# A decoder layer on one core: the mixer's steps regrouped, its last two steps written out with early output products

## The chip, the cores and the metric

The kernel runs on one core of a Trainium2 chip. The metric is the device time of one execution in microseconds. Every time below comes from the time measurements or from one profiled execution.

## The reference, cut to what matters

One decoder layer on x of 4 sequences of 256 tokens with 256 channels: a state-space mixer, an expert layer chosen by token id (weights from ctx), a mixture of 16 experts with two picks a token, each followed by a residual and a layer norm. The change lies in the mixer and its output projection:

```
proj = x @ Win.T                      # per head: x 64, z 64, B 128, C 128 columns, and dt
xc, Bc, Cc = silu(causal_conv(...))   # 4 taps
dt = softplus(dt_raw + dt_bias); decay = exp(-dt * exp(A_log))
h_t = decay_t * h_(t-1) + dt_t * xc_t (x) Bc_t ;  y_t = h_t . Cc_t     # 32 heads
y = y * rsqrt(mean(y * y) + 1e-6) * silu(z)
x = layernorm(x + y.reshape(B, T, 2048) @ Wout.T)
```

## The kernel before, in words

**Work and tiles.** The 32 heads are taken in 16 pairs. A pair n has six tiles of 128 projection channels: tile 0 is x of both heads, tiles 1 to 4 are B and C of the first and of the second head, tile 5 is z. All 1024 tokens run through a tile in two halves of 512. So PE has twelve tiles-and-halves per pair, numbered j = 0 to 11 (in the text: a tile of six matmuls each, since an fp32 product is made of three fp32r products for two slices of 128 channels; `project`, L689). They rotate over four PSUM banks (j % 4).

**Stages.** ACT copies each half out of PSUM times the last tap (`copy`, L1101); DVE adds the other taps from PSUM (`tap`, L1401; three small ones per half in tile 0, two large and two small ones in tiles 1 to 4); a bank is free for tile j + 4 after the tap with shift 3 of that half, which is what `project` waits for (`half_read`). ACT applies silu (L1086), and to the z tile directly from PSUM (L1092). The recurrence is done as products inside chunks: PE turns x to tokens (`x_to_tokens`, L674, four transposes a clump), DVE scales it by dt (`x_scaled`, L1376), PE makes eight scores B C per pair (`score`, L703 and L704), POOL builds the logarithms of the decay (`log_decay`, L421 and L427), ACT exponentiates them (`exp_decay`, L1107), DVE multiplies score and decay (`weigh`, k = 0 to 7, L1385), and PE multiplies that by x (`mix`, L717, four per pair). A score k waits for weigh k - 2, whose bank it uses. The mean of squares: ACT squares (L1112, L1113), POOL makes the low part (`low_part`, L441), PE averages (`mean_square`, L726 and L727, per half g), ACT takes the root (`rsqrt`, L1118 and L1120), DVE applies the gate (`gate`, L1409), POOL normalises into y_all (`norm`, L436).

**Pipeline of steps.** Step n projects pair n (`front`), does x, scores and the mix of the first half for pair q = n - 1 (`mid`), and the second half's mix and both norms for pair r = n - 2 (`tail`). Steps 0 and 1 fill it, steps 2 to 15 have all three (a loop of seven rounds of two), step 16 has mid and tail, step 17 tail alone. Each engine runs its own list in order, and the lists are written out by hand: on PE a dictionary says which other work stands behind which j (L734 to L756), on ACT `work[j]`, on DVE `between[(tile, tap)]`, on POOL the body of `step` (L443). The work between two tiles on PE is a clump below.

**Behind the steps.** SP loads woutT into wo_sb when the last projection is done (L320), the ids and x later (L328, L333). ACT splits the weight into wo_hi (L1176) and makes y_high of pairs 0 to 3 (L1171), DVE finds the owners by id and makes wo_lo (L1557) and y_low of those four (L1562). PE multiplies output blocks 0 and 1 in fp32 (`out_project`, L634), 16 products each, of which the last needs pair 15; then `project_half` makes the blocks 4 to 7 at once from high and low parts (L652, 96 matmuls), six matmuls for each pair i in order. For pairs from 4 on ACT makes y_high and POOL y_low (L506) as it goes. `normed` layer norms, the expert layers and the router follow; they are not touched.

## Time and profile before

| what | us |
|---|---|
| runs shown: median (lowest to highest) of 3 | 718.29 (716.29 to 718.94) |
| the profiled execution: time | 716.46 |
| the profiled execution: span | 714.70 |
| ACT: copy, silu, exponential, one square, Ln and Exp of a root, table load | 0.69, 1.06, 0.84, 0.60, 0.68 and 0.63, 1.28 |
| POOL: log decay of one sequence (two of 0.83, one of 1.29), low part, norm | 2.9, 1.29, 1.29 |
| POOL: split of the next pair's weights | 2.75 and 3.53 |
| POOL: constants, first to last | 4.6 |
| DVE: four y_low (L1562) | 2.5 |

The durations are means of one instruction. A row of the timeline gives the start and the duration in us; a start-to-start distance is the time that an instruction really takes from its engine, since matmuls, and to a small extent the operations of ACT, DVE and POOL, lie over their successors. An fp32 product stands as two records.

### The profile page before, as it was taken

How to read it: one execution, taken by the hardware profiler on the slowest of the kernel's cores; microseconds unless marked ns; L12 is line 12 of the kernel's file. 1: busy time of each engine (PE TensorE's matmuls, PEld its weight loads, DVE VectorE, ACT ScalarE, POOL GpSimd, SP SyncE). 2: the span in 40 equal slices, each digit the busy share in tenths (PEclk: the TensorE clock that was granted, in tenths of full speed). 3: DMA queues.
4: the chain of work that ended last, by engine and by line, in shares of the span. 5: the costliest groups of instructions: out<-in, count | busy, mean ns of one | idle time of the engine just before them, and what ended most of it. 6: DMA issues, size and time to landing. Idle time of an engine off the chain costs nothing.

```text
span 714.7 us, 11631 instructions
## 1 busy us (share of the span) xinstructions
PE 652.1 (91%) x3364; PEld 503.0 (70%) x3364; DVE 539.9 (76%) x856; ACT 451.9 (63%) x744; POOL 478.2 (67%) x452
## 2 busy tenths in 40 slices
PE   6689999999999999999999999899989998999920
PEld 3467777777777777877877777687867775777710
DVE  4879999999999999999999999739525484222236
ACT  3366797797797887877877877865224554333321
POOL 4065887887987888889779876656425758762034
PEclk9899999999999999999999999999999999999975
DMA  4311311311311211112122110320345924543124
GB/s 150 125 46 60 104 46 60 103 45 59 103 45 59 94 54 59 56 66 84 45 63 99 45 59 0 118 95 16 95 118 138 356 73 103 161 136 95 53 74 132
DMA packets 25474, 62.32 MB, mean 87 GB/s; under 512 B 5206, under 2 KB 18134, under 8 KB 22710
## 3 DMA queue, kind: packets, MB, share of 16 engines
q1 hardware_dynamic: 22278, 53.31, 22.1%
q0 software_dynamic: 3168, 8.67, 4.9%
q8 instruction: 14, 0.23, 0.1%
q14 instruction: 14, 0.11, 0.1%
HBM read 52.77 MB, written 9.20 MB: 87 GB/s over the span
## 4 chain that ended last, share of the span: by engine, by line
PE 80%; DVE 7%; POOL 6%; issue 3%; ACT 2%; DMA 2%; POOLq 0%; SPq 0%; DVEq 0%; ACTq 0%
PE ps L689 35%; PE ps L703 8%; PE ps L717 6%; PE ps L934 5%; PE ps L974 4%; PE ps L704 4%; PE ps L634 3%; DVE conv L1401 3%; PE ps L652 2%; POOL conv L599 2%; PE ps L674 2%; PE ps L726 1%; PE ps L952 1%; PE ps L822 1%; PE ps L727 1%
## 5 line engine op out<-in xcount | busy, mean ns | idle before, releaser
L1401 DVE SCALAR_TENSOR_TENSOR conv<-ps,w_raw,conv 128x506 f32<-128x506 f32 (+3 forms) x352 | 324.7, 935 | 19.6 <-ACT conv L1101 13.4
L689 PE MATMUL ps<-x_hi,w_hi 128*128 128x512 f32 x384 | 166.2, 433 | 9.9 <-DVE conv L1401 8.3
L1101 ACT ACTIVATE conv<-ps,w_raw 128x512 f32<-128x512 f32 x160 | 109.8, 687 | 100.2 <-PE ps L689 98.5
L689 PE MATMUL ps<-x_hi,w_lo 128*128 128x512 f32 x384 | 152.1, 396 | 0.0
L689 PE MATMUL ps<-x_lo,w_hi 128*128 128x512 f32 x384 | 151.6, 395 | 0.0
L421 POOL TENSOR_TENSOR decay<-cum_b,cum_tok 128x512 f32<-128x512 f32 (+1 forms) x128 | 103.6, 833 | 24.2 <-DVE cum_tok L1365 24.2
L689 PEld LDWEIGHTS ps<-x_hi,w_hi 128*128 128x128 f32 x384 | 73.3, 191 | 35.1 <-DVE conv L1401 20.5
L427 POOL TENSOR_TENSOR decay<-decay,mask 128x512 f32<-128x512 f32 x64 | 82.8, 1294 | 5.0
L689 PEld LDWEIGHTS ps<-x_hi,w_lo 128*128 128x128 f32 x384 | 72.9, 190 | 16.7
L689 PEld LDWEIGHTS ps<-x_lo,w_hi 128*128 128x128 f32 x384 | 73.5, 191 | 10.3
L703 PE MATMUL ps<-conv 128*128 128x256 f32 x256 | 78.0, 386 | 2.7 <-DVE xs L1376 2.1
L1385 DVE TENSOR_TENSOR decay<-ps,decay 128x384 f32<-128x384 f32 x128 | 69.2, 550 | 14.2 <-PE ps L704 12.4
L1086 ACT ACTIVATE conv<-conv 128x1024 f32<-128x1024 f32 x80 | 79.5, 1064 | 0.0
L441 POOL TENSOR_TENSOR y_lo<-y_sq,y_hi 128x512 fp32r<-128x512 f32 x32 | 41.4, 1292 | 52.6 <-ACT y_sq L1113 52.6
L436 POOL TENSOR_TENSOR y_all<-z_gate,y_all 128x512 f32 (+1 forms) x32 | 41.1, 1285 | 28.6 <-ACT y_all L1120 28.6
L703 PEld LDWEIGHTS ps<-conv 128*128 128x128 f32 x256 | 44.2, 189 | 14.5 <-DVE decay L1385 4.2
L1107 ACT ACTIVATE decay<-decay 128x768 f32<-128x768 f32 x64 | 53.9, 843 | 0.1
L411 POOL TENSOR_TENSOR w_lo<-w_raw,w_hi 128x1536 fp32r<-128x1536 f32 x15 | 52.9, 3529 | 1.2
L704 PEld LDWEIGHTS ps<-conv 128*128 128x128 f32 x256 | 48.6, 190 | 6.7
L717 PE MATMUL ps<-decay,xs 128*64 128x256 f32 (+1 forms) x512 | 49.0, 333 | 1.2 <-DVE decay L1385 1.2
L704 PE MATMUL ps<-conv 128*128 128x128 f32 x256 | 49.2, 274 | 0.0
L717 PEld LDWEIGHTS ps<-decay,xs 128*64 128x64 f32 x512 | 31.7, 136 | 21.7 <-issue 10.6
(233 smaller groups left out, 1065.1 us busy)
## 6 DMA issues: line engine op xcount, KB each, us to landing
cum_b<-cum_scratch SPq DMA_DIRECT2D x16, 1024.0 KB, 4.7
w_raw<-in_winT SPq DMA_DIRECT2D x16, 778.0 KB, 4.3
y_all<-in_wgu SPq DMA_DIRECT2D x4, 1408.0 KB, 19.3
ys_scratch<-y_blk SPq DMA_DIRECT2D x31, 128.0 KB, 1.8
late<-in_wdn SPq DMA_DIRECT2D x2, 1408.0 KB
x_scratch<-conv SPq DMA_DIRECT2D x19, 128.0 KB, 6.6
late<-in_woutT SPq DMA_DIRECT2D x1, 2048.0 KB, 8.3
res_scratch<-conv SPq DMA_DIRECT2D x11, 128.0 KB, 1.9
```

Of the source, the lines that this page charges most:

```text
L411: pool.tensor_tensor(w_lo[:, par, :], raw, w_hi[:, par, :].bitcast(F32), ALU.subtract).then_inc(S["w_split"], 1)
L421: pool.tensor_tensor(decay[:, 2 * b:2 * b + 2, c:t], cum_b[:, qp, :, b * T + j * P:(b + 1) * T], cum_tok[:, 2 * b + j, bass.ds(q * 2, 2)]. ...
L427: pool.tensor_tensor(diag, diag, mask[:, :].unsqueeze(1).unsqueeze(1).broadcast_to([P, 2, 2, P]), ALU.add).then_inc(S["p_arg"], 1)
L689: mm = pe.matmul(ps[:, j % 4, :], wp[:, par, w], xp[:, kk, t], start=(i == 0), stop=(i == 5))
L703: pe.matmul(ps[:, 4 + k % 2, 0:T], Bm[:, c0:c0 + P], Cm[:, c0:c0 + T], start=True, stop=True)
L704: pe.matmul(ps[:, 4 + k % 2, T:SC], Bm[:, c1:c1 + P], Cm[:, c1:c1 + P], start=True, stop=True).then_inc(S["s_done"], 1)
L717: mm = pe.matmul(ps[ch, 6 + g, (b % 2) * T + j * P:(b % 2) * T + T], xs[:, 2 * b + j, ch], decay[:, 2 * b + h, c:t], start=(j == 0), stop= ...
L1086: act.activation(conv[:, pp, tile, :], conv[:, pp, tile, :], ACT.Silu).then_inc(S["a_silu"], 1)
L1101: act.activation(conv[:, par, tile, hf * 512:(hf + 1) * 512], ps[:, j % 4, :], ACT.Copy, scale=w_raw[:, par, tap:tap + 1]).then_inc(S["a_c ...
L1107: act.activation(d, d, ACT.Exp).then_inc(S["a_decay"], 1)
L1385: dve.tensor_tensor(decay[:, k, :], ps[:, 4 + k % 2, 0:SC], decay[:, k, :], ALU.mult).then_inc(S["v_m"], 1)
L1401: dve.scalar_tensor_tensor(out=o[:, :, s:], in0=u[:, :, 0:T - s], scalar=w_raw[:, par, c:c + 1], in1=o[:, :, s:], op0=ALU.mult, op1=ALU.ad ...
```

## The change

- PE's clumps in steps with front: behind j = 0 mean square 0; 1 transposes 0, both mixes of r; 3 transposes 1, mean square 1; 4 scores 0 and 1; 6 score 2; 7 scores 3 and 4; 9 scores 5 and 6, both mixes of q, score 7.
- ACT, DVE and POOL lists of these steps are put in another order to match.
- Steps 16 and 17 get lists of their own. Six of the sixteen products of output blocks 0 and 1 (`project_early`) go between the scores of step 16, with their weights in `wo_early`, a second copy of the first six row blocks of woutT in w_raw's first half, loaded once pair 14 has left it. w_sh's load waits for these products. The other products up to pair 14 stand at the start and in the middle of step 17.
- wo_hi and y_high of pairs 0 to 3 move on ACT into step 16, owners by id and wo_lo on DVE too, and POOL's constants ahead of its step 17. ACT's second of two loads of the logarithm's table there goes.

```diff
+            sp.wait_ge(S["v_tap"], (NPAIR - 1) * TAP_N)
+            sp.wait_ge(S["w_split"], 2 * (NPAIR - 1))
+            sp.dma_start(wo_early, woutT[0:EARLY_WO * P, :].rearrange("(i p) d -> p i d", p=P)).then_inc(S["ld_early"], 16)
...
+            sp.wait_ge(S["eo_done"], 2)
...
+                if isinstance(n, int) and n >= NPAIR:
+                    if mid:
+                        log_decay(n - 1, 1 - par, 2)
+                    low_part(n - 2, 1)
+                    if mid:
+                        log_decay(n - 1, 1 - par, 3)
+                    norm(n - 2, par, 0)
+                    norm(n - 2, par, 1)
+                    if mid:
+                        low_part(n - 1, 0)
+                    return
+                if tail:
+                    low_part(n - 2, 1)
+                    norm(n - 2, par, 0)
                 if mid:
                     log_decay(n - 1, 1 - par, 2)
-                if tail:
-                    low_part(n - 2, 1)
-                if mid:
                     log_decay(n - 1, 1 - par, 3)
-                if tail:
-                    norm(n - 2, par, 0)
                 if split_next:
                     split(n + 1, 1 - par)
+                if mid:
+                    low_part(n - 1, 0)
                 if tail:
                     norm(n - 2, par, 1)
...
+            def project_early(b, first, end):
+                if b == 0 and first == 0:
+                    pe.wait_ge(S["ld_early"], 16)
+                    pe.wait_ge(S["v_tap"], NPAIR * TAP_N)
+                for i in range(first, end):
+                    mm = pe.matmul(ps[:, b, 0:D], y_all[:, i, b * P:(b + 1) * P], wo_early[:, i, :],
+                                   start=(i == 0), stop=False)
+                if end == EARLY_WO:
+                    mm.then_inc(S["eo_done"], 1)
...
-                for j in range(2 * NTILE):
-                    if front:
-                        project(j)
+                def between_tiles(j):
+                    if tail and j == 0:
+                        mean_square(r, 0)
+                    if mid and j in (1, 3):
+                        x_to_tokens(j // 2)
                     if tail and j == 1:
                         mix(r, 2)
                         mix(r, 3)
-                        mean_square(r, 0)
-                        if isinstance(n, int) and n == NPAIR + 1:
-                            pe.wait_ge(S["a_z"], 2 * NPAIR)
-                            out_project(0, 0, NPAIR - 1)
-                    if mid and j in (1, 2):
-                        x_to_tokens(j - 1)
+                    if tail and j == 3:
+                        mean_square(r, 1)
                     if mid:
-                        for k in {3: (0,), 5: (1, 2)}.get(j, ()):
+                        for k in {4: (0, 1), 6: (2,), 7: (3, 4), 9: (5, 6)}.get(j, ()):
                             score(k)
-                    if tail and j == 5:
-                        mean_square(r, 1)
-                    if mid and j == 8:
+                    if mid and j == 9:
                         mix(q, 0)
                         mix(q, 1)
-                    if mid:
-                        for k in {5: (3,), 6: (4,), 9: (5,), 10: (6, 7)}.get(j, ()):
-                            score(k)
+                        score(7)
+                if front:
+                    for j in range(2 * NTILE):
+                        project(j)
+                        between_tiles(j)
+                    return
+                if mid:
+                    x_to_tokens(0)
+                    mix(r, 2)
+                    mix(r, 3)
+                    mean_square(r, 0)
+                    x_to_tokens(1)
+                    project_early(0, 0, EARLY_WO // 2)
+                    score(0)
+                    score(1)
+                    project_early(0, EARLY_WO // 2, EARLY_WO)
+                    score(2)
+                    score(3)
+                    project_early(1, 0, EARLY_WO // 2)
+                    mean_square(r, 1)
+                    mix(q, 0)
+                    score(4)
+                    mix(q, 1)
+                    score(5)
+                    project_early(1, EARLY_WO // 2, EARLY_WO)
+                    score(6)
+                    score(7)
+                    return
+                pe.wait_ge(S["a_z"], 2 * NPAIR)
+                out_project(0, EARLY_WO, NPAIR - 1)
+                mean_square(r, 0)
+                mix(r, 2)
+                mix(r, 3)
+                out_project(1, EARLY_WO, NPAIR - 1)
+                mean_square(r, 1)
...
+                if not front:
+                    if mid:
+                        silu(q, qp, 4)
+                        z(0)
+                        z(1)
+                        act.preload_act_table_set("natural_log_exp_and_others")
+                        exp_decay(0)
+                    square(r, 1)
+                    if mid:
+                        exp_decay(1)
+                    rsqrt(r, 0)
+                    if mid:
+                        exp_decay(2)
+                        exp_decay(3)
+                    rsqrt(r, 1)
+                    if mid:
+                        square(q, 0)
+                        act.wait_ge(S["ld_wo"], 16)
+                        for c in range(4):
+                            part = slice(4 * c, 4 * c + 4)
+                            act.activation(wo_hi[:, part, :], wo_sb[:, part, :], ACT.Copy).then_inc(S["a_wo"], 1)
+                        for i in range(YRING):
+                            high_y(i)
+                    return
                 if mid:
-                    z(0)
-                    work[0] += [lambda: z(1), lambda: silu(q, qp, 4)]
+                    work[0] += [lambda: z(0), lambda: silu(q, qp, 4)]
+                    work[1] += [lambda: z(1)]
                 if isinstance(n, int) and n == 0:
                     work[0] += [lambda: softplus(0)]
                     work[1] += [lambda: softplus(1), lambda: softplus(2)]
                     work[2] += [lambda: softplus(3)]
-                if mid or tail:
-                    work[1] += [lambda: act.preload_act_table_set("natural_log_exp_and_others")]
                 if tail:
                     work[1] += [lambda: square(r, 1)]
-                    work[4] += [lambda: rsqrt(r, 0)]
+                    work[3] += [lambda: rsqrt(r, 0)]
+                if mid:
+                    work[1] += [lambda: act.preload_act_table_set("natural_log_exp_and_others")]
+                    for b, j in enumerate((4, 4, 6, 7)):
+                        work[j] += [lambda b=b: exp_decay(b)]
+                if tail:
                     work[6] += [lambda: rsqrt(r, 1)]
-                if mid:
-                    for b, j in enumerate((1, 2, 7, 8)):
-                        work[j] += [lambda b=b: exp_decay(b)]
-                if front:
-                    work[8] += [lambda: act.preload_act_table_set("silu_and_others")]
+                work[9] += [lambda: act.preload_act_table_set("silu_and_others")]
                 if mid:
                     work[9] += [lambda: square(q, 0)]
...
+                if not front:
+                    if mid:
+                        x_scaled(0)
+                        x_scaled(1)
+                        weigh(0)
+                    gate(r, rp, 1)
+                    if mid:
+                        for k in range(1, 7):
+                            weigh(k)
+                        gate(q, qp, 0)
+                        weigh(7)
+                        owners_by_id()
+                        for c in range(4):
+                            dve.wait_ge(S["a_wo"], c + 1)
+                            part = slice(4 * c, 4 * c + 4)
+                            dve.tensor_tensor(wo_lo[:, part, :], wo_sb[:, part, :], wo_hi[:, part, :].bitcast(F32), ALU.subtract
+                                              ).then_inc(S["v_wo"], 1)
+                    return
                 between = {}
+                if mid:
+                    between[0, 5] = [lambda: x_scaled(0)]
                 if isinstance(n, int) and n == 0:
                     between[1, 0] = [sum_dt]
-                if mid:
-                    between[1, 0] = [lambda: x_scaled(0)]
                 if tail:
                     between.setdefault((1, 0), []).append(lambda: gate(r, rp, 1))
                 if mid:
-                    between[1, 0] += [lambda: x_scaled(1), lambda: weigh(0)]
-                    for k, at_ in ((1, (1, 3)), (2, (2, 0)), (3, (3, 0)), (4, (3, 2)), (5, (4, 0))):
-                        between[at_] = [lambda k=k: weigh(k)]
-                    between[4, 3] = [lambda: gate(q, qp, 0)]
+                    between.setdefault((1, 0), []).append(lambda: x_scaled(1))
+                    for k, at_ in enumerate(((2, 0), (2, 0), (2, 2), (2, 3), (3, 1), (3, 2))):
+                        between.setdefault(at_, []).append(lambda k=k: weigh(k))
                 for m in range(NCONV):
                     for i in range(len(TAPS_OF[m])):
                         for f in between.get((m, i), []):
                             f()
-                        if front:
-                            tap(m, i)
+                        tap(m, i)
                 if mid:
+                    gate(q, qp, 0)
                     weigh(6)
                     weigh(7)
```

## Rows read from the trace of the kernel before

**Rows 1.** The page's totals: busy us, share of the span, instructions.
```profile
PE 652.1 (91%) x3364; PEld 503.0 (70%) x3364; DVE 539.9 (76%) x856; ACT 451.9 (63%) x744; POOL 478.2 (67%) x452
```
**Rows 2.** Stretches: busy us by engine, PEclk, DMA share, GB/s.
```profile
311.40:338.88 27.48, 27.45 (x150) 21.47 (x148) 26.03 (x35) 22.15 (x32) 22.77 (x19) 1.00 0.20 67
455.05:486.92 31.87, 28.62 (x165) 23.19 (x165) 16.07 (x29) 22.53 (x32) 22.49 (x29) 1.00 0.37 119
486.92:510.06 23.14, 22.61 (x96) 18.03 (x97) 17.61 (x29) 8.26 (x16) 16.87 (x15) 1.00 0.03 12
```
**Rows 3.** Waits within one loop step, 311.4 to 338.88: total, times, longest.
```profile
PEld ps L689 <- DVE conv L1401: 0.8, 2, 0.5
```
**Rows 4.** Timeline of PE in a loop step: start, us, operation.
```profile
326.26 0.59 PE L703 MATMUL ps<-conv 128*128 128x256 f32 x2
...
326.83 0.47 PE L689 MATMUL ps<-x_hi,w_hi 128*128 128x512 f32 x1
...
329.67 0.59 PE L703 MATMUL ps<-conv 128*128 128x256 f32 x2
...
330.32 0.60 PE L703 MATMUL ps<-conv 128*128 128x256 f32 x2
...
331.47 0.70 PE L703 MATMUL ps<-conv 128*128 128x256 f32 x2
...
332.15 0.48 PE L689 MATMUL ps<-x_hi,w_hi 128*128 128x512 f32 x1
...
334.19 0.48 PE L689 MATMUL ps<-x_hi,w_hi 128*128 128x512 f32 x1
...
335.44 0.40 PE L689 MATMUL ps<-x_hi,w_lo 128*128 128x512 f32 x1
335.87 0.51 PE L689 MATMUL ps<-x_hi,w_hi 128*128 128x512 f32 x1
...
337.43 1.52 PE L717 MATMUL ps<-decay,xs 128*64 128x256 f32 x16
338.88 0.50 PE L689 MATMUL ps<-x_hi,w_hi 128*128 128x512 f32 x1
```
**Rows 5.** Timeline of DVE in the same step.
```profile
324.59 0.68 DVE L1376 TENSOR_TENSOR xs<-ps,dt_tok 128x512 f32<-128x512 f32 x1
...
332.45 4.01 DVE L1401 SCALAR_TENSOR_TENSOR conv<-ps,w_raw,conv 128x1020 f32<-128x1020 f32 x4
336.38 0.54 DVE L1385 TENSOR_TENSOR decay<-ps,decay 128x384 f32<-128x384 f32 x1
336.85 2.58 DVE L1401 SCALAR_TENSOR_TENSOR conv<-ps,w_raw,conv 128x1020 f32<-128x1020 f32 x2
339.34 0.55 DVE L1385 TENSOR_TENSOR decay<-ps,decay 128x384 f32<-128x384 f32 x1
```
**Rows 6.** DMA issues: KB each, median us to landing.
```profile
late<-in_woutT SPq DMA_DIRECT2D x1, 2048.0 KB, 8.3
```
**Rows 7.** Timeline of PE in the last two steps.
```profile
457.26 0.87 PE L717 MATMUL ps<-decay,xs 128*64 128x256 f32 x8 [1.21 <-DVE decay L1385]
...
478.70 7.50 PE L634 MATMUL ps<-late,y_all 128*128 128x256 f32 x34
```
**Rows 8.** Timeline of ACT and DVE ahead of the half projection.
```profile
480.15 3.88 ACT L1176 ACTIVATE wo_hi<-late 128x1024 fp32r<-128x1024 f32 x4
483.94 2.17 ACT L1171 ACTIVATE y_high<-y_all 128x512 fp32r<-128x512 f32 x4
...
481.29 4.88 DVE L1557 TENSOR_TENSOR wo_lo<-late,wo_hi 128x1024 fp32r<-128x1024 f32 x4 [4.33 <-ACT wo_hi L1176]
```
**Rows 9.** y_low on POOL (chain of waits; by line: ns min/median/max) and DVE beside it.
```profile
491.82 1.30 POOL y_low L506
...
L506 POOL TENSOR_TENSOR y_low<-y_all,y_high x12: 1286/1295/1749, 491.8 to 506.5; 128x512 fp32r<-128x512 f32 x12
...
493.16 1.21 DVE L1499 TENSOR_TENSOR cum_b<-cum_b 128x4 f32<-128x4 f32 x1
```

More of the change, by code:

```diff
@@ L58 @@
 NW = 4
+EARLY_WO = 6
 HALF = NT // 2
@@ L127, in build_layer @@
         y_low = shadow("y_low", [P, NPAIR, NT], y_at)
+        wo_early = w_raw[:, 0, 0:EARLY_WO * D].rearrange("p (i d) -> p i d", i=EARLY_WO)
         xb = sb("xb", [P, NX, D])
@@ L227, in build_layer @@
                  "p_const v_own s_xrank v_xr v_xin p_xpb v_xis s_xtab v_xtok v_xeid v_valid st_x1 "
[L228 removed]
+                 "a_wo v_wo a_yh v_yl p_yl yh_done oh_done a_oh ld_early eo_done v_ve v_root p_root xt1 a_xg hx_done a_sx v_gx gt_done a_gx o1 r1 s1 l1 q1 n1 n1p t1 a_t1 "
                  "lg_done a_lg v_rt v_taken s_rank v_in a_pb p_pb v_is s_tab v_tab v_eid v_meta p_pad "
@@ L475, in _ @@
             step(NPAIR, 0, False, True, True, False)
-            step(NPAIR + 1, 1, False, False, True, False)
             pool.wait_ge(S["p_arg"], NPAIR * 3 * NB)
@@ L502, in _ @@
             clink(pool.memset(goes_on.rearrange("p (e b) -> p e b", b=TBS)[:, :, 0:1], 0.0))
+            step(NPAIR + 1, 1, False, False, True, False)
             for i in range(YRING, NPAIR):
@@ L624, in turn_dt @@
                 pe.wait_ge(S["d_dtT"], 1)
+            def project_early(b, first, end):
[7 more added lines that the diff above has]
+                    mm.then_inc(S["eo_done"], 1)
             def out_project(b, first, end):
-                if first == 0:
+                if end == NPAIR - 1:
                     pe.wait_ge(S["ld_wo"], 16)
@@ L1079, in softplus, with high_y @@
                     act.activation(dt_ch, dt_e, ACT.Ln, bias=1.0).then_inc(S["a_dt"], 1)
+            def high_y(i):
+                act.wait_ge(S["v_y"], 2 * i + 2)
+                if i >= YRING:
+                    act.wait_ge(S["yh_done"], i - YRING + 1)
+                act.activation(y_high[:, i % YRING, :], y_all[:, i, HALF:NT], ACT.Copy).then_inc(S["a_yh"], 1)
             def step(n, par, front, mid, tail):
@@ L1164, in layer_norm_scale @@
                                ).then_inc(S[f"q{i}"], 1)
-            def high_y(i):
-                act.wait_ge(S["v_y"], 2 * i + 2)
-                if i >= YRING:
-                    act.wait_ge(S["yh_done"], i - YRING + 1)
-                act.activation(y_high[:, i % YRING, :], y_all[:, i, HALF:NT], ACT.Copy).then_inc(S["a_yh"], 1)
-            act.wait_ge(S["ld_wo"], 16)
-            for c in range(4):
-                part = slice(4 * c, 4 * c + 4)
-                act.activation(wo_hi[:, part, :], wo_sb[:, part, :], ACT.Copy).then_inc(S["a_wo"], 1)
-            for i in range(YRING):
-                high_y(i)
             layer_norm_scale(0, 0)
@@ L1471, in stat @@
                 dve.wait_ge(S["ln_st"], stats[0])
-            n_x, made = [0], [0]
-            def xlink(*group):
-                for ins in group:
-                    n_x[0] += 1
-                    ins.then_inc(S["v_xr"], 1)
-                dve.wait_ge(S["v_xr"], n_x[0])
+            made = [0]
             def rlink(*group):
@@ L1552, in _ @@
             dve.wait_ge(S["ld_xt"], 16)
-            owners_by_id()
-            for c in range(4):
-                dve.wait_ge(S["a_wo"], c + 1)
-                part = slice(4 * c, 4 * c + 4)
-                dve.tensor_tensor(wo_lo[:, part, :], wo_sb[:, part, :], wo_hi[:, part, :].bitcast(F32), ALU.subtract
-                                  ).then_inc(S["v_wo"], 1)
             for i in range(YRING):
```

28 lines of the change are left out of this document (15 added, 13 removed).

## The prediction, made before the changed kernel ran

> **What bounds the kernel now.** I began with the page's totals [rows 1]: PE is busy 652 of 715 us, the others less. A busy PE may still wait inside, so the stretch table came next [rows 2]. One step of the mixer's loop lasts 27.48 us with PE busy 27.45 of it and DVE 26.03: two engines near the bound at once. The stretch between the loop and the half projection, 455.05 to 486.92, lasts 31.87 us with PE at 28.62, and the half projection 23.14 with 22.61 (PE spans overlap, so real idle is more). The clock is 1.00 in all of them. Third, the waits within a loop step [rows 3]: PE's weight loads stop for DVE's taps, 0.8 us, part of it hidden under matmuls.
>
> **Prices on PE, by start to start** [rows 4]. A score costs 0.65 before another score (329.67 to 330.32) and 0.57 before a tile (326.26 to 326.83); the tile's first matmul gives the 0.08 back. So leaving a clump of scores costs nothing, and two tiles, 326.83 to 329.67 = 2.84, are 0.08 and twice 1.38, or 0.23 a matmul. From 330.32 to 331.47 stand a score (0.57) and a mean square: 0.58, and the score behind it takes 0.68 to the next tile, 0.11 over: 0.69. The two tiles from 334.19 take 3.24 to the mix, 0.40 over: 0.20 is a plain stall, 335.44 to 335.87 for one matmul, since the tap that empties its bank is late; the other 0.20 I split into 0.11 for the restart behind it and 0.09 for going into the mix. The mix runs 1.45 (337.43 to 338.88), with 0.09 ahead and a restart of 0.11 behind 1.65. Eight transposes at 0.11 cost 0.87. Sum of a step: 12 x 1.38 + 8 x 0.65 + 0.87 + 2 x 1.65 + 0.56 + 0.69 = 27.18, with the stall 27.49; measured 27.48.
>
> **The loop after the change, PE.** Same instructions, clumps after tiles 0, 1, 3, 4, 6, 7, 9 instead of 1, 2, 3, 5, 6, 8, 9, 10. Both mean squares leave the scores, so the second costs 0.56; the first stands among matmuls of its own type, which no row shows: between two plain matmuls (0.46) and 0.58, I take 0.50. So PE alone needs 26.95 to 27.05. The saving from fewer clumps is thus small, about 0.15; the rest must come from the stall.
>
> **DVE, walked from PE's start of tile 0 (t = 0).** Prices [rows 5]: a tile of four taps 3.93 (332.45 to 336.38), a weigh 0.47, x_scaled and gate 0.60 each (0.68, of which 0.08 lie over the next, as with the weigh); two large taps followed by a weigh take 2.49 instead of 2.6. PE ends the second transpose clump at 1.38 x 4 + 0.50 + 0.87 + 1.65 = 8.54, and its last transpose, begun 0.11 earlier and 0.27 long, is seen by DVE at 8.75. DVE begins tile 0's taps near 2.5, when ACT's first copy is done; six small taps (0.65 to 0.78), x_scaled and gate bring it to about 8.0. It now waits 0.7 here, where it used to wait for the first score. Then x_scaled 0.60, three tiles 11.79, six weighs 2.8 (0 and 1 ahead of tile 2, 2 and 3 inside it, 4 and 5 inside tile 3), and 3.36 (two taps of 1.31, one of 0.74) up to the tap that frees the bank of the next tile 0, less 0.1 for each of three weighs placed behind a large tap: 8.75 + 18.2 = 27.0. That is also a cycle, through both engines, of 27.0 plus some 0.06 of semaphore time. Halfway, score 4 needs weigh 2, done at 17.3, while PE comes at 17.2: a wait of 0.1 with 0.1 restart. Then PE's remaining work ends the step at 27.2.
>
> **ACT and POOL in the loop.** ACT has 22.2 of 27.5 busy, POOL 22.8 [rows 2]. Squares of the first half now start when the mix clump ends (23.7), the four silus end at 28.6, and the next step's first copy is due at 28.7: no slack, but DVE has the 0.7 above behind it. The two exponentials now sit between the copies of tiles 4 and 5; copy 5 ends at 14.1 and DVE needs it at 14.2. POOL's split of the next weights ends at 24, needed at 27. Neither sets the time, by a few tenths. The gate of the first half moves behind tile 4's taps and ends at 28.2, before the mean square behind the next tile 0 wants it (28.6); behind it the two last weighs end at 28.75 and 29.2.
> A step becomes 27.2, 0.28 less. It is paid in 14 steps (n = 2 to 15; steps 0 and 1 lack the clumps and I cost them at nothing, since there DVE sets the pace): **3.9 us**.
>
> **The last two steps.** Work removed: one of two table loads on ACT. Work moved: the first six of sixteen output products for blocks 0 and 1 run in step 16 from an extra copy of six rows, fetched during step 15 (768 KB; the whole of woutT, 2048 KB, lands in 8.3 us [rows 6]; SP issues it before it waits for the last projections, and only w_sh's load waits for it later). PE from 455.05: wait 1.6 for weigh 6 (28.75 - 27.2; today's mix resumes only at 457.26, [rows 7], since it needs weigh 7 too), transposes 0.87, three mix clumps 4.95, scores 5.2, four mean squares 2.24, 32 products at 0.43 (a block of 34 records takes 7.50, its last one 0.16 of that over its successor) 13.8, ranks 0.45 to 0.9: 29.1 to 29.5, provided PE waits for nothing more. Today it takes 31.87: minus **2.5 us**. Can the others keep up?
> ACT: the split of the weight (3.88) and four y_high (2.17) move ahead of the last square and rsqrt [rows 8]. POOL's queue sets the last exponential (durations in the table above): it is at +6.0 done with the loop's log decays, then come a log decay (2.9), a low part (1.3) and the last log decay (2.9), +13.1; exponential 0.84, rsqrt 1.35 and the square 1.1 end at +16.4, the moved 6.05 at +22.4, and the mix that the second square needs ends only at +23.4: hidden by 1.0. The norm that the last products need is at 23.5 + 1.1 + 1.35 + 1.3 = +27.3, PE comes at +27.9: hidden by 0.6. If that cover went, the excess would land on PE one for one. POOL's constants (4.6) lie between two low parts that are 6 us apart. DVE: score 7 is done at +17.6, the gate and weigh 7 end at +18.7, the owners at +19.5, wo_lo (4.88) at +24.4, the last gate is ready at +24.7; y_low (2.5) then ends near +28, before PE wants it. x_tok's load is not earlier, but no longer blocks wo_lo.
> Then in the half projection y_low of pair 4 runs on POOL from 491.82 to 493.12 [rows 9], because ACT got to y_high only after the second layer norm; PE wanted it at 486.92 + 4 x 1.38 = 492.4. After the change ACT has that done 1.5 us before it is due: minus **0.8**. Bounds of the tail: -3.8 (plus other small waits) to -1 (ACT's cover gone).
>
> **DVE and POOL at once.** On the row, y_low on POOL takes 1286 to 1295 ns but up to 1749, and DVE's operation on 4 columns takes 1.21 beside it [rows 9]: one waits for the other. The change puts DVE's y_low beside POOL's low part and norm, so up to 0.7 of the norm's cover of 0.6 could go; I count 0.1. The Trainium skill, "SBUF — State Buffer", section "Who interferes with whom", says that a DVE instruction with two SBUF inputs contends with a GpSimd instruction that reads SBUF and the second fully blocks. By it the sum would be at most 0.7 worse, and in the loop nothing changes, as DVE's operations there have a PSUM input; the trace agrees.
>
> **Sum.** 3.9 + 2.5 + 0.8 = 7.2 us. Everything behind the half projection is the same chain, shifted. The profiled execution took 716.46 (span 714.70); it becomes 709.3. It lies 1.8 under the median of the three runs, 718.29, against which I forecast **711.1 us**.
>
> **Rivals.**
> A. The loop is no shorter: a wait on DVE (score 4, or x_scaled's 0.7) eats the 0.3. For: PE and DVE both need over 26 of 27.48, and my walk's slacks are 0.1. Against: its sum for today is right to 0.01. Only the tail stays: 718.3 - 3.3 = 715.0. 20%.
> B. The waits at score 4 vanish and the loop runs at PE's own 26.96: 14 x 0.52 + 3.3 = 10.6 less: 707.7. 16%.
> C. Slower: the pair of exponentials, now directly ahead of copy 5, delivers it late, DVE's tile 2 starts late, and so the tap that frees the next step's bank. The cycle is 27.0 + (delay - 0.1). At 1.0 late (one exponential and its wait) with the rest as above a step is 28.0: + 7.3 - 3.3, 722.3. It costs more than the tail gives from 0.8 late on. For: 0.1 of slack there; against: ACT has 5 us idle in the step. 8%.
> D. The loop gains, the tail does not: ACT's moved 6.05 us lie on the path to the last norm (if the first square is over 1 us later than walked, a late exponential being enough). 718.3 - 3.9 = 714.4. 6%.
> The forecast itself, loop 27.1 to 27.3 with a tail of 2.5 to 3.8 less: 50%.
>
> **Numbers.** From these: 706.0 to 716.5 leaves out C, the far end of B and the top of A. 0.5% is 3.6 us, about what can be told from no change. Faster than 714.7: the forecast, B, and part of A and D, 0.70; within: the rest of A and D, 0.21; slower than 721.9: 0.09, C and what I did not think of.
>
> **What the changed profile would show.** A step of 27.2 from one mix clump to the same one in the next; DVE waiting some 0.7 for the transposes, nowhere for scores; no matmul start of 0.43 inside the tiles. The half projection 29.3 after the loop's end and 22.2 long. Wrong would be: a step at or above 27.4, DVE waiting for ACT's copies of tile 2, PE idle over 1 us ahead of the last products, or a half projection that starts when wo_lo or y_low ends.

## The result, and the profile after

After the change the kernel takes **711.35 us** (median, 710.15 to 714.67) beside 717.28 us before (716.29 to 720.79): ratio 0.992, 95% interval 0.9893 to 0.9947, so 0.5 to 1.1% faster. The profiled execution took 711.14 us, its span 709.41 where the one before had 714.72. The page's totals, then the stretch table with the stretches of [rows 2]: a loop step, loop end to half projection, half projection:
```profile
PE 648.2 (91%) x3364; PEld 511.5 (72%) x3364; DVE 538.2 (76%) x856; ACT 454.0 (64%) x743; POOL 477.9 (67%) x452
```
```profile
340.93:368.23 27.30, 27.19 (x149) 22.03 (x148) 25.65 (x35) 22.36 (x32) 22.77 (x19) 1.00 0.20 68
450.17:479.25 29.08, 27.68 (x166) 22.56 (x165) 18.40 (x31) 21.49 (x32) 22.80 (x30) 1.00 0.40 131
479.25:501.62 22.37, 22.37 (x99) 18.11 (x98) 18.77 (x27) 8.67 (x17) 18.11 (x16) 1.00 0.04 12
```
27.30 for 27.48, 29.08 for 31.87, 22.37 for 23.14: all three stretches shrank as forecast, the step least. The loop ends 4.88 us earlier, the half projection 8.44 us earlier (501.62 for 510.06). But the program ends only 5.31 earlier. Of the lost 3.1 us some 2.7 are in two stretches behind, which the stretch table of the changed kernel shows (PEclk, the granted clock, is the third figure from the end; the page's own clock row is the same before and after, its slices are too wide for them):
```profile
526.40:529.77 3.37, 2.93 (x9) 2.47 (x10) 0.08 (x1) 0.84 (x3) 2.46 (x4) 0.50 0.45 111
563.90:567.30 3.40, 3.40 (x12) 2.35 (x11) 2.69 (x27) 1.59 (x5) 0.41 (x1) 0.50 0.72 251
```
TensorE was granted 0.50 there, 1.2 instead of 2.4 GHz. Against the same instructions of before the lead is 8.4 us from the half projection to the first looked-up context and 8.07 at the second, for which PE waits 1.20 instead of 0.85; then it falls to 6.9 across the first stretch and to 5.3 across the second, and stays within 0.2 elsewhere. The first stretch begins inside that wait. PE's timeline:
```profile
517.84 5.97 PE L849 MATMUL ps<-cum_b,ident 128*128 128x384 f32 x18
525.20 0.44 PE L868 MATMUL ps<-ident,conv 128*128 128x128 f32 x2 [1.40 <-DMA conv<-x_scratch,cum_b]
526.84 0.69 PE L868 MATMUL ps<-ident,conv 128*128 128x128 f32 x2 [1.20 <-DMA conv<-x_scratch,cum_b]
```
L849 are filler matmuls, eleven calls, that keep PE busy until the contexts of the first lookup arrive. They come 8.4 us earlier too, and the contexts 1.4 us behind them. Before had about the same gap (1.37 and 0.85) and no slower stretch there, but one of 3.4 us at 42.2, in step 1, that this execution lacks. So single executions differ in what the clock does, which the experiments had to take apart.

**The loop step.** DVE and PE in the step from 340.93. First DVE's timeline:
```profile
349.78 0.69 DVE L1467 TENSOR_TENSOR xs<-ps,dt_tok 128x512 f32<-128x512 f32 x1 [0.88 <-PE ps L700]
350.38 4.01 DVE L1492 SCALAR_TENSOR_TENSOR conv<-ps,w_raw,conv 128x1020 f32<-128x1020 f32 x4
354.32 1.01 DVE L1476 TENSOR_TENSOR decay<-ps,decay 128x384 f32<-128x384 f32 x2
355.25 2.58 DVE L1492 SCALAR_TENSOR_TENSOR conv<-ps,w_raw,conv 128x1020 f32<-128x1020 f32 x2
357.74 0.55 DVE L1476 TENSOR_TENSOR decay<-ps,decay 128x384 f32<-128x384 f32 x1
```
and PE's:
```profile
357.42 0.59 PE L729 MATMUL ps<-conv 128*128 128x256 f32 x2
357.85 0.38 PE L730 MATMUL ps<-conv 128*128 128x128 f32 x2
358.35 0.70 PE L729 MATMUL ps<-conv 128*128 128x256 f32 x2
358.88 0.38 PE L730 MATMUL ps<-conv 128*128 128x128 f32 x2
359.02 0.47 PE L715 MATMUL ps<-x_hi,w_hi 128*128 128x512 f32 x1
```
A score costs 0.65 before another [rows 4], 0.43 of it for L729 (357.42 to 357.85), so 0.22 for L730. Here score 4 starts 0.50 behind 357.85, because the third weigh ends at 358.29: a stall of 0.28, and its own L729 takes 0.53 instead of 0.43: 0.10 of restart. That 0.385 (by the full decimals) is all that PE waits for another engine in the step; without it the step would take 26.92.

**The last two steps.** PE waits once, then never again until the half projection:
```profile
451.73 0.63 PE L700 MATMUL ps<-ident,conv 128*128 128x128 f32 x4 [1.41 <-ACT conv L1148]
```
and the end of what DVE has left of the loop:
```profile
451.04 1.01 DVE L1476 TENSOR_TENSOR decay<-ps,decay 128x384 f32<-128x384 f32 x2
```
PE's row names ACT's silu, but these transposes want only the first of five silus that begin at 447.76 with 1.06 each. The other thing that the code waits for there is the seventh weigh, the first of the two in DVE's row, 0.55 long: it ends at 451.59. So the wait is the one forecast. ACT, DVE and POOL in order of time:
```profile
466.40 3.89 ACT L1208 ACTIVATE wo_hi<-late 128x1024 fp32r<-128x1024 f32 x4
470.19 2.18 ACT L1141 ACTIVATE y_high<-y_all 128x512 fp32r<-128x512 f32 x4
473.67 0.60 ACT L1174 ACTIVATE y_hi<-ps 128x512 fp32r<-128x512 f32 x1 [1.30 <-PE ps L743]
```
```profile
469.61 4.63 DVE L1519 TENSOR_TENSOR wo_lo<-late,wo_hi 128x1024 fp32r<-128x1024 f32 x4
475.46 4.15 DVE L1647 TENSOR_TENSOR y_low<-y_all,y_high 128x512 fp32r<-128x512 f32 x4
```
```profile
476.13 1.73 POOL L442 TENSOR_TENSOR y_all<-z_gate,y_all 128x512 f32<-128x512 f32 x1
479.62 1.30 POOL L442 TENSOR_TENSOR y_all<-z_gate,y_all 128x512 f32<-128x512 f32 x1 [1.75 <-ACT y_all L1182]
```
Where before DVE's part of the weight's split ended at 486.17 [rows 8] and PE waited 0.4 for the y_low behind it, ACT's part now ends 9 us (470.3) and DVE's 5 us (474.2) ahead of the half projection, and ACT waits 1.30 behind y_high. Two things are close. The first norm ends at 477.86, 0.13 ahead of the products that want it (477.99), and y_low ends at 479.61, 0.36 behind the half projection's start and still ahead of its first use of the fourth part (from 479.25 + 3 x 1.38 = 483.4 on).

### The profile page after: what moved, and what is told of

Its sections match the earlier page's. It is cut to its first block, busy times and chain, and to the rows that moved or that the text cites. A ratio compares the mean times of both kernels' runs of the same rounds, so it can differ in the third digit from the quotient of the medians.

```text
span 709.4 us, 11617 instructions
## 1 busy us (share of the span) xinstructions
PE 648.2 (91%) x3364; PEld 511.5 (72%) x3364; DVE 538.2 (76%) x856; ACT 454.0 (64%) x743; POOL 477.9 (67%) x452
## 4 chain that ended last, share of the span: by engine, by line
PE 69%; DVE 12%; issue 6%; ACT 5%; POOL 4%; DMA 2%; SPq 0%; POOLq 0%; DVEq 0%; ACTq 0%
PE ps L715 26%; DVE conv L1492 7%; PE ps L743 7%; PE ps L989 5%; PE ps L729 5%; PE ps L1029 4%; PE ps L660 3%; PE ps L678 3%; ACT decay L1169 3%; DVE decay L1476 2%; PE ps L730 2%; POOL conv L614 2%; PE ps L700 2%; PE ps L877 1%; PE ps L1007 1%
## 5 line engine op out<-in xcount | busy, mean ns | idle before, releaser
L1492 DVE SCALAR_TENSOR_TENSOR conv<-ps,w_raw,conv 128x506 f32<-128x506 f32 (+3 forms) x352 | 320.4, 933 | 17.5 <-ACT conv L1163 12.8
L715 PE MATMUL ps<-x_hi,w_hi 128*128 128x512 f32 x384 | 159.1, 414 | 10.0 <-DVE conv L1492 8.6
L1163 ACT ACTIVATE conv<-ps,w_raw 128x512 f32<-128x512 f32 x160 | 108.1, 686 | 71.7 <-PE ps L715 71.5
L715 PEld LDWEIGHTS ps<-x_hi,w_hi 128*128 128x128 f32 x384 | 72.6, 189 | 28.6 <-DVE conv L1492 10.2
L729 PE MATMUL ps<-conv 128*128 128x256 f32 x256 | 79.5, 392 | 1.8 <-DVE decay L1476 0.3
L1476 DVE TENSOR_TENSOR decay<-ps,decay 128x384 f32<-128x384 f32 x128 | 67.6, 547 | 7.8 <-PE ps L730 7.7
L1169 ACT ACTIVATE decay<-decay 128x768 f32<-128x768 f32 x64 | 52.0, 837 | 4.0 <-POOL decay L433 3.9
L730 PEld LDWEIGHTS ps<-conv 128*128 128x128 f32 x256 | 48.6, 190 | 6.6
L729 PEld LDWEIGHTS ps<-conv 128*128 128x128 f32 x256 | 43.3, 189 | 12.7 <-DVE decay L1476 4.2
L730 PE MATMUL ps<-conv 128*128 128x128 f32 x256 | 49.2, 274 | 0.0
L415 POOL TENSOR_TENSOR w_hi<-w_raw,zero 128x1536 fp32r<-128x1536 f32 x15 | 41.2, 2746 | 8.5 <-DVE w_lo L1415 8.5
## 6 DMA issues: line engine op xcount, KB each, us to landing
y_all<-in_wgu SPq DMA_DIRECT2D x4, 1408.0 KB, 19.4
```

Of the source, the lines that this page charges most:

```text
L715: mm = pe.matmul(ps[:, j % 4, :], wp[:, par, w], xp[:, kk, t], start=(i == 0), stop=(i == 5))
L729: pe.matmul(ps[:, 4 + k % 2, 0:T], Bm[:, c0:c0 + P], Cm[:, c0:c0 + T], start=True, stop=True)
L730: pe.matmul(ps[:, 4 + k % 2, T:SC], Bm[:, c1:c1 + P], Cm[:, c1:c1 + P], start=True, stop=True).then_inc(S["s_done"], 1)
L1163: act.activation(conv[:, par, tile, hf * 512:(hf + 1) * 512], ps[:, j % 4, :], ACT.Copy, scale=w_raw[:, par, tap:tap + 1]).then_inc(S["a_c ...
L1169: act.activation(d, d, ACT.Exp).then_inc(S["a_decay"], 1)
L1476: dve.tensor_tensor(decay[:, k, :], ps[:, 4 + k % 2, 0:SC], decay[:, k, :], ALU.mult).then_inc(S["v_m"], 1)
```

## The experiments

The first four kernels (loop_only to late_split in the table) ran on a chip where the kernel before takes 731.4 us and split_tap on one with 732.0, the others on chips with 717.5 to 717.8. All compute the reference's whole output. The table holds profiled executions, one a kernel: a step (start to start of its projection, mean of ten), step 1, loop end (start of step 15 plus its length) to half projection, length of that up to the end of its last matmul (0.16 more than in the stretch table), what lies behind, and how long PE was granted 0.50 behind the half projection (the last some 30 us, which all have, left out). No trace of the kernel before was taken on the chips with 731 to 732 us, so what lies behind cannot be compared for the five kernels there.

| kernel | step | step 1 | to half | half | behind | at 0.50 |
|---|---|---|---|---|---|---|
| before | 27.475 | 28.10 | 31.84 | 23.30 | 204.5 | 0 |
| after | 27.303 | 25.90 | 29.08 | 22.54 | 207.6 | 3.4 + 3.4 |
| loop_only | 27.302 | 27.19 | 33.68 | 23.29 | 219.7 | 13.6 |
| tail_only | 27.496 | 26.85 | 29.54 | 22.50 | 223.4 | 20.4 |
| no_early | 27.304 | 25.92 | 34.27 | 22.53 | 217.9 | 6.8 |
| late_split | 27.300 | 27.16 | 35.94 | 24.92 | 220.5 | 17.0 |
| after_ctl | 27.317 | 25.95 | 29.06 | 22.55 | 207.2 | 3.4 + 3.4 |
| weigh2_early | 27.333 | 26.79 | 29.07 | 22.50 | 204.9 | 0 |
| turn_early | 27.329 | 25.90 | 29.06 | 22.55 | 204.4 | 0 |
| warm15 | 27.308 | 25.93 | 29.08 | 22.50 | 205.9 | 0 |
| tile1_first | 27.340 | 25.79 | 29.06 | 22.55 | 204.9 | 0 |
| tile1_warm15 | 27.353 | 25.75 | 29.08 | 22.50 | 205.0 | 0 |
| warm5 | 27.305 | 25.91 | 29.04 | 22.55 | 211.0 | 6.8 + 10.2 |
| split_tap | 27.307 | 26.41 | 29.06 | 22.51 | 222.6 | 23.8 |

**loop_only**: the kernel before with the loop's new order alone.
```
 def step(n, par, front, mid, tail):
-    (order of before in the loop)
+    (order of after in the loop)
     (steps 16 and 17, weight split, constants, products: as before)
```


> The new lists for the steps with projections (n = 0 to 15), the old ones for steps 16 and 17 and all behind. Theory: a loop step lasts 27.30 us as in the changed kernel, the half projection starts 31.9 us after the loop's end as before and lasts 23.1; the time is 2.4 us under before in schedule, plus or minus some 1.7 us for each stretch in which TensorE's granted clock is at half that comes or goes. Rival (the two parts lean on each other): the tail starts later than 31.9 after the loop, since weighs 6 and 7 end 0.1 to 0.5 later against the projections.

730.82 us, ratio 0.9992 (0.9977 to 1.0006). The step is after's, so the loop gives 0.17 a step, not 0.28. But the rival held: the old tail starts its half projection 1.84 us later behind the loop's end: the new order leaves POOL's log decays of the first part to the end of the step, done 6.2 us behind it instead of 4.35, and PE meets waits of 0.44 and 1.68 for xs. Loop alone: nothing to be measured.

**tail_only**: the last steps alone, the loop as before.
```
-    (order of after in the loop)
+    (order of before in the loop)
     (steps 16 and 17 as after)
```


> The old lists for n = 0 to 15, the new ones for steps 16 and 17 and all behind. Theory: 27.48 us a step, half projection starts 29.1 us after the loop and lasts 22.4: 3.5 us under before in schedule, plus or minus 1.7 us for each stretch at half clock. Rival (the tail's gain was given back behind the half projection by something other than the clock, say the gathers or the loads): the span behind the half projection is some 3 us longer than before, with the clock at 1.00 throughout.

728.40 us, ratio 0.9959 (0.9945 to 0.9974). The step is before's, the tail nearly after's: 29.54. The tail's steps are worth 2.3 to 2.8 us here and 0.8 in the half projection, and with either loop; the new loop pays in full only with the new tail, since the old one gives back 1.84 of its 2.4 us. The rival, a loss behind the half projection at full clock, is not settled here: this execution has 20.4 us at half clock there, and no trace of before was taken on its chip. turn_early below settles it: the same tail, full clock, and 204.4 us behind, as before.

**no_early**: after without the early products and their load.
```
-    project_early(0, 0, EARLY_WO // 2)      (and three more)
-    out_project(0, EARLY_WO, NPAIR - 1)
+    out_project(0, 0, NPAIR - 1)
```


> The changed kernel without the twelve early products and their load; all 15 products of blocks 0 and 1 stand in step 17. Theory: PE had waits in step 16 that they filled, though only in part, so the half projection starts 32.6 us after the loop instead of 29.1. Rival (PE is full in step 16 anyway and the products are only moved): it starts at 29.1 to 29.5.

728.51 us, ratio 0.9972 (0.9935 to 1.001), so by time alone not shown to differ from before. The half projection starts at +34.27, 5.2 us later than in after. The products fill PE's waits of step 16, which are back:
```profile
457.71 0.67 PE L725 MATMUL ps<-conv 128*128 128x256 f32 x2 [0.72 <-DVE decay L1468]
460.14 0.50 PE L748 MATMUL ps<-y_hi,mean_w 128*128 128x512 f32 x1 [1.54 <-POOL y_lo L443]
```
and in the stretch that begins 0.8 us behind the second wait the clock is halved:
```profile
460.90:464.30 3.40, 3.40 (x16) 2.12 (x18) 0.33 (x1) 1.27 (x2) 3.24 (x4) 0.50 0.02 3
```
Half of 3.4 us, 1.7, is the difference to the expected figure of 32.6. So some 3.5 of the 5.2 us are PE's waits, of which the two rows show 2.3, and the rest is clock.

**late_split**: after with wo_hi and y_high on ACT, and wo_lo on DVE, behind step 17.
```
-    square(q, 0); act.wait_ge(S["ld_wo"], 16); wo_hi x4; high_y x4    (step 16)
+    wo_hi x4; high_y x4; layer_norm_scale(0, 0)                       (behind step 17)
```


> The changed kernel with wo_hi and the first four y_high back behind step 17 on ACT, and wo_lo behind it on DVE. Theory: the chain rsqrt, wo_hi, wo_lo, y_low sets the start of the half projection again; it starts 36.0 us after the loop (29.1 + 6.9) and lasts 23.1, so moving the split is what lets the early products pay. Rival (the split was not on the path, only PE's products were): 29.1 to 30.

733.12 us, ratio 1.003 (1.0012 to 1.0049): slower than before. The start at +35.94 is the expected one; PE waits 6.73 for y_low, and from 483.3, inside that wait, to 493.5 the clock is halved: 5.3 us of the half projection, which so is 24.92 long:
```profile
488.22 0.77 PE L678 MATMUL ps<-y_high,wo_hi 128*128 128x512 f32 x1 [6.73 <-DVE y_low L1647]
```
ACT's split starts at +29.3 here, where before it started at +25.1: it stands behind a last root that the new order of PE makes later. The moved split is the part that the whole tail hangs on. What it saves is that wait and the clock that falls in it.

**after_ctl** and three moved operations. after_ctl is after, unchanged, so that the two clock stretches can be seen to repeat.

> The changed kernel again, on the chip of its variants below. Expected: 27.30 us a loop step, the half projection 29.1 us after the loop; stretches at half clock in other places than in the first profile if they hang on the moment and not on the kernel, in the same places (526 and 564 us) if they hang on its gaps alone.

710.38 us, ratio 0.9914 (0.9887 to 0.994), with stretches of 3.4 us at 526.9 and 564.5 again: not an accident of one execution. Its gap is 1.31 and 0.92 us, and what lies behind the half projection is 2.7 us longer than before, which is what the two stretches take by themselves.

**weigh2_early** moves the third weigh ahead of tile 2's second tap:
```
-    enumerate(((2, 0), (2, 0), (2, 2), (2, 3), (3, 1), (3, 2)))
+    enumerate(((2, 0), (2, 0), (2, 1), (2, 3), (3, 1), (3, 2)))
```


> The changed kernel with weigh 2 one large tap earlier on DVE (ahead of the second tap of tile 2). Theory (the wait at score 4, 0.39 us a step, is the term I sized too small, and it hangs on weigh 2): the wait goes, DVE's tap that frees the next tile 0's bank binds at 27.0 plus 0.1, a step takes 27.05 to 27.15, 2.1 to 3.5 us less in all. Rival (PE's stall only moves to the next tap in DVE's chain): 27.25 to 27.3.

712.51 us, ratio 0.9937 (0.9906 to 0.9968), step 27.33: the theory fell. Score 4 no longer waits, the projection half behind it does (it starts 0.48 behind the score's second pair, with 0.34 for its first matmul):
```profile
360.88 0.38 PE L730 MATMUL ps<-conv 128*128 128x128 f32 x2
361.36 0.50 PE L715 MATMUL ps<-x_hi,w_hi 128*128 128x512 f32 x1
```
```profile
PEld ps L715 <- DVE conv L1492: 0.3, 1, 0.3
```
The waiting for a tap of tile 2 was there all along, in the shadow of score 4.

**turn_early** has besides the second transposes one projection half earlier, so that DVE need not wait 0.88 for them:
```
-    if mid and j in (1, 3): x_to_tokens(j // 2)
+    if mid and j in (1, 2): x_to_tokens(j - 1)
```


> As weigh2_early, and the second transpose clump behind tile 2 instead of tile 3 on PE, so that DVE does not wait 0.9 us for it. Theory (the cycle through transposes, x_scaled and the last tap is what is left): DVE's chain starts when ACT's copy 3 is there, 0.35 earlier, and PE alone binds: 26.9 to 27.0 a step, 4.5 to 5.5 us less than the changed kernel. Rival (PE's own 26.95 was underestimated or DVE's chain is not in the way): the same as weigh2_early.

710.76 us, ratio 0.9921 (0.9887 to 0.9956), step 27.33. DVE scales x at once, and then waits for what comes next, ACT's copy 3 of a half that PE now ends later:
```profile
349.08 0.68 DVE L1467 TENSOR_TENSOR xs<-ps,dt_tok 128x512 f32<-128x512 f32 x1
350.66 4.03 DVE L1492 SCALAR_TENSOR_TENSOR conv<-ps,w_raw,conv 128x1020 f32<-128x1020 f32 x4 [0.90 <-ACT conv L1163]
```
**tile1_first** starts from after again (x scaled behind the first tap of tile 1, table load of ACT behind copy 3):
```
-    between.setdefault((1, 0), []).append(lambda: x_scaled(1))
+    between[1, 1] = [lambda: x_scaled(1)]
-    work[1] += [lambda: act.preload_act_table_set(...)]
+    work[3].insert(0, lambda: act.preload_act_table_set(...))
```


> After, with the step's wait attacked where turn_early left it: VectorE's first tap of tile 1 starts when ScalarE's copy 3 ends, so (1) VectorE scales the second half of x behind that tap instead of ahead of it, and (2) ScalarE preloads the logarithm's table behind copy 3 instead of ahead of copies 2 and 3. Theory (the tap of tile 2 for which projection half 8 waits ends a gap-free VectorE chain that starts with that tap of tile 1): the tap starts at about +9.0 of the step instead of +9.4, the waits of 0.385 us a step go, the step falls from 27.32 to 26.95-27.05 us and the loop ends 4 us earlier. Rival (TensorE waits elsewhere, the second score for the x that is now scaled later): step 27.2-27.35. Everything behind the loop as in after.

710.11 us, ratio 0.9899 (0.9856 to 0.9942), step 27.34. DVE starts the tap at the end of copy 3 but 0.2 later than it started x_scaled before, and the same work stands behind:
```profile
350.11 1.28 DVE L1492 SCALAR_TENSOR_TENSOR conv<-ps,w_raw,conv 128x1020 f32<-128x1020 f32 x1 [1.05 <-ACT conv L1163]
```
**split_tap** is tile1_first with 15 fillers and with that tap cut in two:
```
 TAPS_OF = [... if m == 0 else
+    [(slice(0, 1), 1), (slice(1, 2), 1), (slice(0, 2), 2), (slice(0, 1), 3), (slice(1, 2), 3)] if m == 1 else
```


> tile1_warm15 with the first tap of tile 1 as two of half its width: VectorE can do the first half from ScalarE's copy 2, in the 1.05 us in which it now waits for copy 3, then scales x, then does the second half. Theory (VectorE's chain from copy 3 to the tap of tile 2 that projection half 8 waits for sets the 0.37 us of waits a step; tile1_first failed because its chain held the same work from about the same start): the chain is 0.8 us shorter, the waits at the fifth score, the second score and half 8 go, the step falls from 27.35 to 26.95-27.05 us, the loop ends about 4.5 us earlier and the total is 703-706 us. Rival (the waits are TensorE's for something beside this chain, or VectorE's work of 0.2 us more a step eats it): step 27.2-27.4, total 708-710. Behind the loop as in tile1_warm15.

724.29 us beside 732.03, ratio 0.9889 (0.9866 to 0.9911), step 27.31. DVE's chain is 0.5 us shorter up to tile 2, and all of it is given back there. DVE's rows and ACT's:
```profile
356.31 2.59 DVE L1493 SCALAR_TENSOR_TENSOR conv<-ps,w_raw,conv 128x1020 f32<-128x1020 f32 x2 [0.20 <-ACT conv L1164]
```
```profile
351.01 1.28 ACT L1224 ACT_TABLE_LOAD   x1
...
354.13 1.57 ACT L1170 ACTIVATE decay<-decay 128x768 f32<-128x768 f32 x2
355.60 0.68 ACT L1164 ACTIVATE conv<-ps,w_raw 128x512 f32<-128x512 f32 x1
```
The taps of tile 2 now wait for copy 5, and copy 5 for the two exponentials ahead of it, which the moved table load made late. Reckoned from PE's third projection half, the third weigh starts at 11.61, 11.65 and 11.60 us in after, tile1_first and split_tap: three different waits, one time. The version that is left, the cut tap with the table load where after has it, was not tried; so whether PE's own 26.9 can be had stays open.

**warm15** has 15 calls of the filler instead of 11 (line 848), **warm5** five, **tile1_warm15** is tile1_first with 15.

> The changed kernel with 15 instead of 11 filler matmuls ahead of the gathered blocks, so that PE works until they land. Theory (the half clock ahead of the first gathered blocks came from PE's 2.6 us of idleness there): no stretch at half clock within 10 us behind the fillers; that place is 1.5 us shorter than in a profile that has it. Rival (the fall hangs on what PE does later, on short transposes and products): it is still there, and the kernel is up to 0.2 us longer.

> After with 5 instead of 11 filler matmuls: TensorE idles about 5.5 instead of 2.6 us ahead of the first gathered context. Theory (the clock falls because TensorE idles there, and 2.6 us is at the edge): half-clock stretches behind the gap in this kernel too, of more length than after's two of 3.4 us, and behind the half projection 208-211 us, total 711-715. Rival (the stretches come from somewhere else, or from chance): none or the same two, and a total within 0.5% of after.

> tile1_first with 15 instead of 11 filler matmuls ahead of the gathered contexts, so that TensorE does not idle there. Theory: step 26.95-27.05 and no half-clock stretch behind the gathers, so a time of about 705 us, below both kernels. Rival: step 27.2-27.35, about 708.5 us as with 15 fillers alone.

Measured: warm5 712.92 us (ratio 0.9929, 0.9904 to 0.9955), after_ctl 710.38, warm15 708.87 (0.991, 0.9876 to 0.9944), tile1_warm15 709.11 (0.9882, 0.9844 to 0.9921). In warm5 PE idles 5.2 us, and both stretches are longer; warm15 has no gap and full clock. First warm5, then warm15:
```profile
522.80:529.60 6.80, 3.96 (x12) 3.01 (x13) 0.42 (x1) 1.53 (x4) 5.23 (x6) 0.50 0.39 101
563.80:574.00 10.20, 10.20 (x31) 7.76 (x30) 4.43 (x39) 3.02 (x10) 0.73 (x2) 0.50 0.18 62
```
```profile
523.50:530.00 6.50, 6.26 (x30) 4.42 (x29) 0.84 (x2) 2.32 (x7) 4.73 (x5) 1.00 0.41 108
```
Behind the half projection: 211.0, 207.6 and 205.9 us with 5, 11 and 15 calls. More idling in front of the gathers (the lookups), more time at half clock: the theory held in these executions, and the granted clock of all runs goes the same way, 0.967 with 5 calls (median of 12 runs), 0.972 in after_ctl (10), 0.974 in warm15 (5). With 11 calls it goes either way: before, weigh2_early, turn_early and tile1_first have gaps of 1.3 to 1.6 us like after and no stretch behind, which is worth 2 to 3 us there; what decides between them was not found. The intervals of these kernels overlap after's, so none is shown to be faster than after by total time; by median warm15, on the same chip, is 1.5 us below after_ctl, and tile1_warm15 1.0 below tile1_first, its own chip's kernel with 11. The chip with 732 us halves the clock in split_tap with 15 calls too (at 535.5 and 569.6).

## Why the prediction was right, and where not

The forecast was 711.1 us and a ratio of 0.990; measured were 711.35 and 0.992. Its total is closer than its terms:

| term | predicted | measured |
|---|---|---|
| 14 loop steps | -3.9 | -2.4 |
| steps 0 and 1 | 0 | -2.45, of it about 1.25 clock, 0.25 spread |
| loop end to half projection | -2.5 | -2.8 |
| half projection | -0.8 | -0.8 |
| behind | 0 | +3.1: 2.7 clock, 0.4 a later lookup |
| span | -7.2 | -5.3 |

That the total came out is luck. The loop gave 1.5 us too little, steps 0 and 1 gave 1.2 that was not counted, the tail 0.3 more: 7.2 again. In the profiled pair the clock and the later lookup then took 3.1 behind, and the clock gave 1.25 in step 1. And the forecast stood on a median of 718.29 for the kernel before, of three runs, where the seven of the result have 717.28: the gain in medians is 5.9 us, not 7.2.

**The loop: mechanism right, one term too small.** PE alone was put at 26.95 to 27.05 and needs 26.92. DVE waits 0.88 for the transposes (forecast 0.7), the mean square among its own type costs 0.46. The step that failed is "a wait of 0.1 with 0.1 restart" at score 4: it is 0.28 with 0.10. The walk had the third weigh done at 17.3 and it was, at 17.36; it had PE there at 17.2, and PE would have been there at 17.14. So two errors of 0.06 and the semaphore's time left out made a wait of 0.1 three times as long: 0.385 with its restart for 0.2, less 0.08 that PE alone needed less, is 0.10 a step, the missing 1.5 us.
The stall is not one place but a tie. Rival B, the loop at PE's own 26.96, was given 16% on the idea that the waits might vanish; the four kernels that went at these waits had steps of 27.31 to 27.34. And rival C's place, copy 5 behind the exponentials, is real, though not in after: there copy 5 ends at 354.89 and DVE wants it at 355.25, 0.36 of slack for the forecast 0.1. In split_tap it binds.

**Steps 0 and 1 were costed at nothing, "since there DVE sets the pace".** That failed: step 1 is 2.2 us shorter. Before's has the slow stretch at 42.2. tail_only has the old step without one: 26.85, so 1.25 is clock and 0.95 the new order. The 0.25 of step 0 is no gain of the order: with the old one step 0 takes 29.80 in before and 29.50 in tail_only, with the new one 29.55 in after. Of the kernels with the new order those with such a stretch need 26.4 to 27.2 and those without 25.75 to 25.95, which agrees. What is saved are PE's waits. The old step 1 (tail_only) waits for the scaled x and for a weigh, the new one (after) for a tap and a weigh:
```profile
49.18 0.67 PE L731 MATMUL ps<-conv 128*128 128x256 f32 x2 [1.07 <-DVE xs L1471]
54.63 0.67 PE L731 MATMUL ps<-conv 128*128 128x256 f32 x2 [0.48 <-DVE decay L1480]
```
```profile
53.42 0.50 PE L715 MATMUL ps<-x_hi,w_hi 128*128 128x512 f32 x1 [0.30 <-DVE conv L1492]
58.05 0.67 PE L729 MATMUL ps<-conv 128*128 128x256 f32 x2 [0.28 <-DVE decay L1476]
```
1.55 against 0.58 accounts for the 0.95.

**The last two steps: as walked.** First transposes at +1.56 (forecast 1.6), the weight's split and y_high hidden by 1.30 (1.0), wo_lo from +19.4 to +24.1 (19.5 to 24.4), start at +29.08 (29.1 to 29.5). That POOL's queue, not ACT, sets the last exponential held (POOL's log decay ends at +13.3 for 13.1). late_split shows the price of the cover: 6.9 us later. What no single row could say is that loop and tail depend on each other: loop_only's tail is 1.84 us longer, so the parts do not add up, and the new tail hides what the new loop does to POOL.

**Contention was undersized and hidden.** Counted was 0.1, with 0.7 as the worst. DVE's y_low took 4.15 us beside POOL's low part and norm, where before, alone, the same four took 2.48, and a norm 1.73 instead of 1.3. One by one, the first y_low began at 475.46, inside POOL's low part (to 476.18), and took 1.27 instead of 0.68; the norm began at 476.13, inside it, and took 1.73; the second y_low began at 476.65, inside the norm (to 477.86), and took 1.76; the last two, alone, took 0.68 each. So each time the one that came second waited for the first. The rule of the Trainium skill, "SBUF — State Buffer", section "Who interferes with whom", is that a DVE instruction with two SBUF inputs contends with a GpSimd instruction that reads SBUF, and that the order of issue decides who blocks; this trace agrees. That cost DVE 1.7 and POOL 0.4: y_low ended 1.4 later than forecast (near +28; it was +29.4) and PE still did not want it, but of the norm's cover of 0.6 only 0.13 was left.

**Behind the half projection "the same chain, shifted"** is the sentence that cost most. It holds for the instructions: in executions with no slow stretch there it takes 204.4 to 205.0 us (205.9 in warm15) beside before's 204.5. It does not hold for the clock: PE waits for the gathers as it did before, and in after and after_ctl the clock falls behind that wait, where in before it did not.

## What to carry to other kernels

Where two engines tie within a few tenths, price a stall by the latest of all paths that end near it, not by the one that the trace shows; take the shown wait away in thought and look for the next before counting the gain. Where fillers end ahead of what they cover, as the eleven calls here did by 1.4 us before and after, the clock may fall in one execution and not in another: look at the granted clock of each stretch before comparing two kernels by one profile, and over all runs before choosing the number of fillers. Parts of one change can be worth nothing alone (the loop order) or carry the others (the weight split), so undo them one by one before keeping or dropping them.

## What was not expected of the hardware

A gap of PE of some 2.6 us (1.40 and 1.20 with two transposes between) was followed by 3.4 us at 1.2 GHz, begun inside its second part, and, 34 us later, with no gap over 1.0 us between, by another 3.4 us; a gap of 5.2 us by 6.8 and 10.2 us. The later stretch came wherever the earlier one was (after, after_ctl, warm5) and never without it on those chips. The first cost 1.1 us, the later 1.6. The gap alone does not decide: 1.31 and 0.92 in after_ctl with a stretch, 1.61 and 0.83 in tile1_first with none. Why either comes is open. The lead that the change had won shrank by 2.7 us through these two, half of what the span gained.
